# A new order in the prologue, earlier loads at the end of attention, and the first expert's chunks in pairs

## The reference

```python
def xattn(hc, hq, w_sim, b_sim, W_qv, b_qv):     # hc = layernorm(x), hq = ctx
    w1, w2, w3 = w_sim[:d], w_sim[d:2*d], w_sim[2*d:]
    Sim = (hc @ w1)[:, :, None] + (hq @ w2)[:, None, :] + einsum('bid,bjd->bij', hc * w3, hq) + b_sim
    hq_hat = einsum('bij,bjd->bid', softmax(Sim, 2), hq)
    hc_bar = einsum('bi,bid->bd', softmax(max(Sim, 2), 1), hc)      # pooled sum over all rows
    return concatenate([hc, hq_hat, hc * hq_hat, hc * hc_bar], -1) @ W_qv + b_qv

def ffn(x, ...):                                 # 8 experts, top 2, capacity 640 rows each
    gates = softmax(x @ w_router + b_router); topv, topi = top_k(gates, 2)
    buf = scatter rows to their experts, in order, as long as there is room
    out = gelu(buf @ w1 + b1) @ w2 + b2          # w1: 512 x 2048, w2: 2048 x 512 per expert
    return sum of the two experts' rows, weighted by the gates

x = x + tanh(g_xattn) * xattn(layernorm(x), ctx, ...)
x = x + tanh(g_ffn) * ffn(layernorm(x), ...)
```

## Time and profile before

| | us |
|---|---|
| median of 3 runs | 2213.1 (2212.66 to 2215.7) |
| the profiled execution | 2215.85 |
| its span in the trace | 2214.1 |
| PE busy in it | 2163.2 |

### The profile page before, as it was taken

The page is one execution under the profiler, slowest core; times in us unless marked ns, Lnnn a source line. Parts: engine busy times, 40 slices in busy tenths (PEclk is TensorE's granted clock), DMA queues, the critical chain, the costliest instruction groups (busy, mean ns, idle before and its releaser), DMA issues.

```text
span 2214.1 us, 34539 instructions
## 1 busy us (share of the span) xinstructions
PE 2163.2 (98%) x12061; PEld 1123.4 (51%) x12061; DVE 1305.7 (59%) x2729; ACT 1149.4 (52%) x1773; POOL 144.8 (7%) x141
## 2 busy tenths in 40 slices
PE   4999999999999999999999999999999999999997
PEld 2444444444444444444455545556556565647464
DVE  7755566555566655654666787655646464646450
ACT  6765555565555655555534346535445353526260
POOL 0000000000000000000012222010101010010101
PEclk9999999999999999999999999999999999999999
DMA  9534444443444443444878965443333334343411
GB/s 252 133 80 106 108 111 100 115 98 89 108 108 105 109 113 86 94 98 116 186 202 246 250 172 156 114 108 105 100 109 95 109 95 114 90 125 116 122 41 24
DMA packets 485237, 266.13 MB, mean 120 GB/s; under 512 B 424388, under 2 KB 424772, under 8 KB 481084
## 3 DMA queue, kind: packets, MB, share of 16 engines
q1 hardware_dynamic: 474156, 244.90, 42.5%
q0 software_dynamic: 11024, 20.52, 4.8%
HBM read 97.96 MB, written 71.52 MB: 77 GB/s over the span
## 4 chain that ended last, share of the span: by engine, by line
PE 94%; DMA 2%; ACT 1%; DVE 1%; SPq 1%; issue 1%; POOL 0%; ACTq 0%; POOLq 0%; DVEq 0%
PE ps L1325 23%; PE ps L1341 22%; PE ps L2138 18%; PE ps L2123 16%; PE ps L1784 11%; PE ps L2108 1%; DMA arena<-arena 1%; PE ps L455 1%; PE ps L1792 1%; DMA arena<-in_ctx 1%; PE ps L2150 0%; PE ps L1805 0%; DVE arena L850 0%; SPq L337 0%; PE ps L1337 0%
## 5 line engine op out<-in xcount | busy, mean ns | idle before, releaser
L1325 PE MATMUL ps<-arena 128*128 128x512 f16 (+1 forms) x2688 | 554.1, 356 | 7.1 <-DMA arena<-arena 5.0
L1341 PE MATMUL ps<-arena 128*128 128x512 f16 x2400 | 553.1, 379 | 2.2 <-DMA arena<-arena 2.2
L2138 PE MATMUL ps<-arena 128*128 128x512 f16 x1872 | 407.0, 380 | 2.8 <-issue 2.8
L1325 PEld LDWEIGHTS ps<-arena 128*128 128x128 f16 x2688 | 249.3, 98 | 285.8 <-DMA arena<-arena 5.7
L1341 PEld LDWEIGHTS ps<-arena 128*128 128x128 f16 x2400 | 233.5, 98 | 278.1 <-DMA arena<-arena 2.7
L2123 PE MATMUL ps<-arena 128*128 128x320 f16 x2688 | 366.3, 299 | 0.0
L1148 ACT ACTIVATE arena<-ps,arena 128x512 f32<-128x512 f32 (+1 forms) x224 | 163.6, 732 | 388.0 <-PE ps L1325 388.0
L2123 PEld LDWEIGHTS ps<-arena 128*128 128x128 f16 x2688 | 263.0, 98 | 103.2
L2138 PEld LDWEIGHTS ps<-arena 128*128 128x128 f16 x1872 | 183.5, 98 | 223.9 <-issue 5.3
L879 DVE SCALAR_TENSOR_TENSOR arena<-arena 128x512 f16<-128x512 f32 x192 | 144.1, 750 | 186.8 <-ACT arena L1169 186.8
L866 DVE TENSOR_REDUCE arena<-arena 128x1 f32<-128x512 f32 (+1 forms) x224 | 139.8, 625 | 192.7 <-ACT arena L1148 191.9
(11 more groups left out here) (252 smaller groups left out, 1524.8 us busy)
## 6 DMA issues: line engine op xcount, KB each, us to landing
arena<-in_L_ffn_w SPq DMA_DIRECT2D x64, 1024.0 KB, 8.9
feats<-arena SPq DMA_DIRECT2D x48, 512.0 KB, 2.8
arena<-in_x SPq DMA_DIRECT2D x32, 512.0 KB, 3.5
rows<-arena SPq DMA_DIRECT2D x13, 774.0 KB, 3.8
out<-arena SPq DMA_DIRECT2D x16, 512.0 KB, 3.3
arena<-in_ctx SPq DMA_DIRECT2D x6, 1024.0 KB, 13.2
arena<-arena SPq DMA_TRANSPOSE x276, 3.0
arena<-in_L_xattn_W_qv SPq DMA_DIRECT2D x4, 1024.0 KB, 5.7
```

Source lines behind the costliest of these rows:

```text
L1325: mm = pe.matmul(out, qT[:, q, s * KD + k, :], ctxT[:, r * KD + k, a:z], start=(k == 0 and s + r == 0), stop=(k == KD - 1 and s == 1))
L1341: mm = pe.matmul(psO[q], turned, ctxN[:, j, r, :], start=(j + s + r == 0), stop=False)
L2138: mm = pe.matmul(psO[:, t % 2, :], hT[:, f, s, t * P:(t + 1) * P], w2s[:, r, f * D:(f + 1) * D], start=(f + s + r == 0), stop=(f == KF - 1 ...
```

## The change

It has three parts.

1. **Prologue.** SP loads all of the context first, w1, the bias and x of block 1 behind it. PE turns six tiles (`PET = 6`) instead of four, tiles 4 and 5 with a copy on DVE and on ACT, and DMA the other 20. Both queries are turned early, into banks of their own (`psQ` is now two), and unit 1's first chunk is scored before unit 0's. The table `FIRST` is new, so the 14 first score chunks come in another order, and the orders on ACT, DVE and PE are written anew around it. `norm_lo(0)` and `norm_hi(0)` move to the front; `tail_low` moves ahead of the last seven maxima of the row maximum of unit 0.
2. **End of attention.** The top matmul of the pooled sum and `total_top` move from chunk 4 to chunk 5 of the last unit, `total_weight` to the last chunk, on ACT and DVE. On SP the loads of W_qv go one chunk forward, and the features and x of block 0 stand ahead of P transpose 4 instead of behind it and the store.
3. **First expert.** Two chunks share one multiplication for the high half (128 x 640 elements instead of twice 128 x 320) and one low half, in both halves of its first layer. The buffers `h32` hold a pair each, and a `Gelu` waits for the low half of two pairs back. All four maxima of W2 stand in the first half, with the low halves of chunks 6 to 13, and the high parts come earlier. In the last block, `turn_rows`, the router and the counts stand one or two chunks of the first expert later. PE's second half uses four PSUM banks instead of two.

The arithmetic of the matmuls is unchanged, and so is their number. The core of the diff:

```diff
@@ FirstHalf.gelu, low
-        if f >= 2:
-            act.wait_ge(self.lo, f - 1)
-        act.activation(self.h32[f % 2][:, half], self.psA[f % 4], ACT.Gelu, ...
-        act.wait_ge(self.g_done, f + 1)
-        act.mul(self.hT[:, f, 0, half], self.h32[f % 2][:, half], ew.sh[:, 0:1]).then_inc(self.hi, 1)
+        if f % 2 == 0 and f >= 4:
+            act.wait_ge(self.lo, f - 2)
+        buf = self.h32[f // 2 % 2]
+        act.activation(buf[:, f % 2 * self.HALF:(f % 2 + 1) * self.HALF], self.psA[f % 4], ACT.Gelu, ...
+        if f % 2:
+            act.wait_ge(self.g_done, f + 1)
+            act.mul(self.hT[:, f - 1:f + 1, 0, half], buf.rearrange("p (f i) -> p f i", f=2), ew.sh[:, 0:1])\
+               .then_inc(self.hi, 2)
@@ attention
-    FIRST = ((0, 1, 2, 3, 5, 7, 8), (4, 6, 9, 10, 11, 12, 13))
+    FIRST = ((1, 2, 4, 5, 8, 9, 10), (0, 3, 6, 7, 11, 12, 13))
+    MAXES0 = 11
+    PET = 6
@@ sync, body
             for c in range(NC):
+                if last and c == 0:
+                    sp.wait_ge(qk_done, NC * U)
+                    mg.load_weights(sp, 2)
                 turn_p(u - 1, c)
-                if last and c in (1, 2):
-                    if c == 1:
-                        sp.wait_ge(qk_done, NC * U)
-                    mg.load_weights(sp, c + 1)
+                if last and c == 1:
+                    mg.load_weights(sp, 3)
+                if last and c == 3:
+                    load_first()
...
                 if c == 4 and not first:
                     store_f(u - 3, 1)
-                if last and c == 4:
-                    load_first()
@@ sync, prologue
-        for j in range(TC, JT):
+        for j in range(PET, JT):
             turn_ctx(j)
@@ vector, body
                 if last and not i:
-                    if c == 4:
+                    if c == 5:
                         total_top()
-                    if c == 5:
+                    if c == LAST:
                         total_weight()
@@ tensor, body
-                if last and not i and c == 4:
+                if last and not i and c == 5:
                     pe.wait_ge(hc_step, HK * U)
...
                     pe.matmul(psX, tz[:, 0:1].broadcast_to([P, P]), identf, start=True, stop=True)
@@ tensor, prologue
         pe.wait_ge(made, 3)
         sums(0)
         sums(1)
+        pe.wait_ge(eye, 1)
+        turn_query(0, psQ[0])
         sums(2)
         turn(0)
         turn(1)
+        turn(2)
+        turn_query(1, psQ[1])
+        turn(3)
         sums(3)
+        turn(4)
+        turn(5)
         pe.wait_ge(q0_ready, QT)
         first_scores(1, 0)
+        sums(4)
+        first_scores(0, 0)
...
@@ vector, merge_and_route
+        fh.low(dve, 0)
+        route_1_of(NB - 1)
+        fh.low(dve, 2)
+        route_2_of(NB - 1)
+        for f in range(4, ew.KF, 2):
             fh.low(dve, f)
-            if f in (10, 13):
-                ew.max_part(dve, 1, (f - 10) // 3)
+            if 6 <= f <= 12:
+                ew.max_part(dve, 1, (f - 6) // 2)
@@ tensor, last_chain
             fh.chunk(pe, 0)
+            counts(NB - 2)
             fh.chunk(pe, 1)
             pe.wait_ge(y_step, YK * (NB - 1) + YQ[1])
+            fh.chunk(pe, 2)
             turn_rows(NB - 1, (NB - 1) % NR)
-            fh.chunk(pe, 2)
-            counts(NB - 2)
             fh.chunk(pe, 3)
+            fh.chunk(pe, 4)
             router(NB - 1)
-            for f in range(4, 6):
+            for f in range(5, 8):
                 fh.chunk(pe, f)
             counts(NB - 1)
@@ experts
-    HIGHS, LOWS = (4, 5, 7, 8, 10, 11, 13, 14), (5, 6, 8, 9, 11, 12, 14, 15)
+    HIGHS, LOWS = (1, 3, 4, 5, 7, 8, 9, 11), (2, 3, 5, 5, 7, 9, 9, 11)
@@ experts, tensor, second_half
-                if f >= 2:
-                    pe.wait_ge(g_done, f - 1)
+                if f >= 4:
+                    pe.wait_ge(g_done, f - 3)
...
-                        mm = pe.matmul(psH[:, f % 2, 1, :], ...
+                        mm = pe.matmul(psH[:, f % 2, f // 2 % 2, :], ...
```

More of the change, by code:

```diff
@@ L539, in attention @@
     psT = [ps[:, 6 + n, :].bitcast(F16).rearrange("p (k i) -> p k i", i=P) for n in range(2)]
-    psQ = ps[:, 3, :].bitcast(F16).rearrange("p (k i) -> p k i", i=P)
+    psQ = [ps[:, 3 - n, :].bitcast(F16).rearrange("p (k i) -> p k i", i=P) for n in range(2)]
     psY_first = ps[:, 2:4, :]
@@ L709, in sync @@
         load_ctx(1)
-        sp.dma_start(w1b, w_sim[0:D].partition_broadcast(P)).then_inc(w1_loaded, 16)
-        sp.dma_start(bs, b_sim.partition_broadcast(P)).then_inc(w1_loaded, 16)
-        load_ctx(2)
-        load_x(1)
-        for c in range(3, NC):
+        for c in range(2, NC):
             load_ctx(c)
@@ L1123, in split_high, with turned @@
                            bias=zero[:, 0:1], scale=gscale[:, 2 * p // TC:2 * p // TC + 1]).then_inc(c_hi, 1)
+        def turned(j):
+            act.wait_ge(ct_done, j + 1)
+            act.copy(ctxT[:, :, j * P:(j + 1) * P], psT[j % 2]).then_inc(ct_out[j % 2], 1)
         def query_high(u, q, row, ready):
@@ L1206, in half @@
                     query_high(2 * b + 2 + c // 3, c // 3, row0, RK * (2 * b + 2 + c // 3) + 2)
-                if last and not i and c == 5:
+                if last and not i and c == LAST:
                     total_weight()
@@ L1220, in scalar @@
         norm_sd(0)
+        norm_hi(0)
         squares(0)
@@ L1223, in scalar @@
         squares(1)
+        query_high(1, 1, rowbuf[1], 4)
+        squares(2)
         split_high(0)
-        squares(2)
         split_high(1)
+        act.wait_ge(q0_done, 1)
+        act.copy(qT[:, 0], psQ[0]).then_inc(q0_ready, 1)
         split_high(2)
@@ L1313, in first_scores @@
             n = FIRST[q][c]
-            if c:
-                pe.wait_ge(ct_turned[c], 16 * (TILES[c][1] - TILES[c][0]))
+            a, z = TILES[c]
+            for v in range(2):
+                pe.wait_ge(ct_out[v], min(z, PET) // 2)
+            if z > PET:
+                pe.wait_ge(ct_turned[c], 16 * (z - max(a, PET)))
             if n >= 4:
@@ L1976, in second_half @@
             half = slice(HALF, CAP)
-            for f in range(KF):
-                if f < 2:
-                    ew.max_part(dve, 1, f + 2)
-                if f == 3:
+            for f in range(1, KF, 2):
+                if f == 1:
                     ew.scales(dve, 1, True)
-                if f in LOWS:
-                    ew.low_part(dve, 1, LOWS.index(f), True)
+                for n in range(CH):
+                    if LOWS[n] in (f - 1, f):
+                        ew.low_part(dve, 1, n, True)
                 if f == 7:
@@ L1987, in second_half @@
                 dve.wait_ge(h_hi, f + 1)
-                dve.scalar_tensor_tensor(out=hT[:, f, 1, half], in0=h32[f % 2][:, half], scalar=sh[:, 0:1],
-                                         in1=hT[:, f, 0, half], op0=ALU.mult, op1=ALU.subtract).then_inc(h_lo, 1)
+                dve.scalar_tensor_tensor(out=hT[:, f - 1:f + 1, 1, half],
+                                         in0=h32[f // 2 % 2].rearrange("p (f i) -> p f i", f=2), scalar=sh[:, 0:1],
+                                         in1=hT[:, f - 1:f + 1, 0, half], op0=ALU.mult, op1=ALU.subtract)\
+                   .then_inc(h_lo, 2)
         def layer_1(e):
```

173 lines of the change are left out of this document (82 added, 91 removed).

## The result

| | before | changed |
|---|---|---|
| median, 6 runs each | 2214.97 us (2212.66 to 2218.66) | 2205.42 us (2204.42 to 2206.88) |
| span of the profiled execution | 2214.1 us | 2203.7 us |

The ratio is 0.9956, with a 95% interval of 0.9944 to 0.9968: 9.6 us less by the medians, 10.4 us by the spans. The forecast of 2203.0 started from the first three runs of before, whose median was 2213.1; the three that came later took 2214.66 to 2218.66.

A forecast was written before the change was run, and what follows sets the result against it. TensorE was taken to bound the kernel, busy 2163.2 of 2214.1 us, so only its waits could go. Gains of 2.0, 2.2 and 6.0 us, 10.2 off the median 2213.1, gave 2203.0 us, range 2200.3 to 2208.5.

The forecast's parts named there:

- The sum: Whole kernel: 2.0 in the prologue, 2.2 at the end of attention and 6.0 in the first expert, 10.2 us off.
- Prologue: 2.0 forecast: Up to PE's third score chunk in the loop: Exp table loaded 2.1 us earlier, chunk near 78.9, 2.0 us won.
- the last transpose: Prologue: the last DMA transpose of the context ends at 55.3 us, from 1.39 us spacing.
- VectorE's order: Prologue: the tail's copy, waiting for the last transpose, stands ahead of seven maxima, so the row maximum ends at 59.8 us.
- End of attention: 2.2 forecast: Last attention products: waits of 1.34 and 2.20 us removed, 0.15, 0.7 and 0.5 new, 2.2 us won.
- the two charged waits: End of attention: PE waits 0.7 us for P transpose 4 and 0.5 us for P transpose 5.
- Rival 2: End of attention: features delay P transposes 4 and 5 by 3 to 5 us, total 2205 to 2208; chance 0.12.
- First expert: 6.0 forecast: First expert's first layer and second layer: 4.3 us, and 1.7 more if the clock stays up, 6.0 us won.
- The 1.7 of the clock: First expert's second layer: without the wait ahead of it, the clock stays up and 1.7 us more is won.
- Rival 1: New idle stretches at the loop's entry or second half: clock falls at one place, costing 1.7 us, 2204.7; chance 0.22.

The follow-up runs named there:

- p_pro: The kernel before with only the prologue part of the change; median 2212.36 us, ratio 0.9988.
- x_pairs: The changed kernel with pairs kept, but W2's maxima, scales, high and low parts back at their old places; median 2210.88 us, ratio to before 0.9981.
- t_counts: The changed kernel with PE's counts of the last block one chunk earlier, behind chunk 6; median 2204.58 us, ratio to before 0.9954.
- p_att: The kernel before with only the end-of-attention part of the change; median 2212.25 us, ratio 0.9990.
- p_exp: The kernel before with only the first-expert part of the change; median 2210.65 us, ratio 0.9983.
- x_w2: The kernel before with single chunks, but W2's four maxima in the first half and its high and low parts earlier; median 2210.46 us, ratio 0.9978.
- att_sum: The kernel before with the pooled sum alone moved one chunk on, SP's order the old one; 2213.35 us, one time.
- att_sp: The kernel before with SP's new load order alone, the top matmul staying at chunk 4; 2213.0 us, one time.
- t_tail: The changed kernel with the tail's copy on DVE behind unit 0's row maximum instead of ahead of the seven maxima; median 2203.82 us, ratio to before 0.9950.
- best_warm: `best` with an Exp activation on a constant between the evictions of chunks (0, 5) and (0, 6); median 2205.03 us, ratio to before 0.9952.
- best: The changed kernel with the tail's copy behind the row maximum and the counts one chunk earlier; median 2201.72 us, ratio to before 0.9940.
- best_warm_max: `best_warm` with W2's maxima behind pairs 8 to 14 and high and low parts from chunk 3; median 2204.49 us, ratio to before 0.9951.

## Why the prediction was right

**The sum.** Forecast 10.2 us off the profiled span, measured 10.4; the median 2205.42 lies in the range of 2200.3 to 2208.5, 2.4 us above the point. 1.9 of these come from the median from which I subtracted, 2213.1 of three runs and 2214.97 of six. The mechanism was right in each part: the waits that I named went, and new ones came where I put them. That the sum hits 10.4 within 0.2 is partly luck. The prologue gave 0.7 us less than forecast and the end of attention 1.0 more, and the profile of before that I took as the base had the longest wait for transpose 5 of four and a fall of the clock that not every run has. By the medians it is 9.6 us.

**Prologue: 2.0 forecast, 1.3 measured.** The step that was too short is the last transpose: 55.3 forecast, 56.6 measured, because the first was issued at 26.10 and not 25.5, and they came 1.43 us apart and not 1.39. Then tail and maxima took 4.2 us, as worked out, and the row maximum 0.4 and not 0.3. The table was loaded at 61.23, 0.7 us and not 2.1 ahead of before, and the chain behind it was 18.4 us instead of 19.0. Over four profiles with the new prologue (the changed kernel, `p_pro`, `x_pairs`, `t_counts`) and six with the old (before, `p_att`, `p_exp`, `x_w2`, `att_sum`, `att_sp`) A lies at 1046.60 and 1048.16 in the mean, 1.6 us apart. PE had the first scores done at 63.5, 6.2 us earlier than before, where I had 7.8. That most of this would come back was right: as new waits of 3.68 and 0.28 us, forecast 4 and 2.7, and as 1.6 us of slow clock between them, which took the place of most of the second wait. So was its cause: `t_tail` shows 2.2 us more behind VectorE's order.

**End of attention: 2.2 forecast, 3.2 in the first profile, 2.4 over all.** Eight profiles with the new code took 36.04 to 37.40 us from A to B (mean 36.5; the longest is `best_warm`), four with the old 37.94 to 39.58 (mean 38.9). The term that I had mis-sized is the two charged waits, 0.7 and 0.5 us. Counted from A, since all of this stands 1.3 us earlier than before, the features were issued 0.8 us later than I had it and held SP for 6.20 us and not 7.28. So transpose 4 was issued at 26.0 and not 26.3 and landed at 30.3 and not 30.7, and 0.25 us of waiting was left. That is chance in part: in `p_att` the features' issue took 7.11 us and PE waited 0.78. Rival 2, that the features hold the transposes up by 3 to 5 us, came in none of the eight; the most was 0.98 us of waiting, in `best_warm`.

**First expert: 6.0 forecast, 5.9 measured**, 4.22 from C to D and 1.68 from D to E. The wait for rows was 2.55 us, where I had 2.4, and the second layer started without a wait. `x_pairs` and `x_w2` show that each edit alone would have left 1.4 to 3 us. I had worked out 57.1 us from C to D, and it was 57.15. The 1.7 of the clock were less sure than I put them: behind the wait of 2.8 us ahead of the second layer the clock fell in three of five profiles (before, `p_pro`, `p_att`) and did not in `att_sum` and `att_sp`, so over many runs its end is worth about 1.0 us, an estimate from these five.

**Rival 1, the clock falls elsewhere.** At the loop's entry it fell in each of four profiles with a wait of 3.7 us there, and took 1.3 to 2.8 us. As I said, PE has to wait again before the third chunk anyway, so nothing to 0.4 us of it reached that chunk. At the first expert's rows it fell in `p_exp` (2.57 us) and in `best_warm` (2.94), for 1.4 and 1.6 us, and not in the changed kernel (2.55) nor in five others (1.2 to 2.5). The Trainium skill (TensorE: Matmul & The Clock Gate, Part 1) says that the gate halves the rate after idleness and that the number of slow matmuls varies from run to run. The rows agree with both. By idle time alone, though, the 3.35 us in `x_pairs` would sooner have cost clock than the 1.00 in `att_sum`, and it was the other way round.

## What to carry to other kernels

A copy that waits for a late transfer should stand behind the work that the critical chain needs, in the order of an engine's own queue: 0.3 us of copy at the wrong place held seven maxima and cost 2.2 us. Where an engine's idle time ends on a result that several engines hand on, follow that chain to the last engine that waits for an instruction placed too late (here the counts: 1.26 us on DVE gave 1.0 at the end). Before a gain is read off one profile, look at how much the same stretch of unchanged code differs among profiles; here the wait for one DMA transpose alone went from 0.6 to 2.2 us. And a wait that a profile doesn't show may only be hidden: in `att_sum` PE came late to a transpose that would otherwise have held it.

## What was not expected of the hardware

The clock of TensorE fell to the 1.2 GHz level behind a wait of 1.00 us and ten matmuls of one column in one profile, and stayed at 2.4 GHz behind 3.35 us in another: how long PE was idle does not alone say whether it falls. An indirect DMA on POOL takes 0.97 us alone or beside a maximum on VectorE, and 1.07 to 1.62 when it begins inside a low half, ending 0.85 us after it, in the changed kernel, `best` and `best_warm_max`.
